# Attention and routed feed-forward layer: transposes in two steps, reciprocals spread by transfers, first scores in the projection stage

## The reference

```python
def xattn(Q, K, V):                       # Q = layernorm(x), K = V = context
    q = split_heads(Q @ Wq.T + bq); k = split_heads(K @ Wk.T + bk); v = split_heads(V @ Wv.T + bv)
    scores = einsum('bhqd,bhkd->bhqk', q, k) / sqrt(8)
    return merge(softmax(scores) @ v) @ Wo.T + bo
def ffn(xf):
    expert_idx = argmax(xf @ Wr.T + br)
    h = relu(einsum('td,efd->etf', xf, W1) + b1)
    y = einsum('etf,edf->etd', h, W2) + b2
    return y[expert_idx, arange(tokens)]
x = x + xattn(layernorm(x), ctx, ctx)
x = x + ffn(layernorm(x))
```

## Time and profile before

| | us |
|---|---|
| median of 3 runs | 499.29 (499.02 to 500.56) |
| the profiled execution, its own time | 501.58 |
| its span, first to last instruction | 499.8 |
| busy: PE, DVE, ACT, POOL | 461.1, 408.2, 313.0, 240.6 |

### The profile page before, as it was taken

How to read it: one execution, slowest core, us unless ns; L and a number is a source line. 1 busy time by engine, 2 the same in 40 slices (tenths; PEclk the granted TensorE clock), 3 DMA queues, 4 the chain that set the end, 5 groups by cost and what they waited for, 6 DMA issues and landing times. The chain is left out here.

```text
span 499.8 us, 18728 instructions
## 1 busy us (share of the span) xinstructions
PE 461.1 (92%) x6467; PEld 347.9 (70%) x6467; DVE 408.2 (82%) x1061; ACT 313.0 (63%) x589; POOL 240.6 (48%) x390
## 2 busy tenths in 40 slices
PE   3999978899999999999999999988789999999990
PEld 1666634456666666666666666668779999999990
DVE  4999864677899899998999999958878887887870
ACT  1677764666666666666666665665557777777760
POOL 1548620222232464555645645554767645455551
PEclk9999995999999999999999999999999999999996
DMA  8356300011000111111111115722223332222100
GB/s 281 108 148 177 90 11 12 14 22 20 18 17 18 33 41 30 38 38 36 35 34 33 39 41 201 264 71 76 77 66 103 101 87 66 72 61 74 39 32 0
DMA packets 32752, 33.98 MB, mean 68 GB/s; under 512 B 6675, under 2 KB 26006, under 8 KB 32416
## 3 DMA queue, kind: packets, MB, share of 16 engines
q1 hardware_dynamic: 27840, 24.10, 18.7%
q0 software_dynamic: 4832, 8.80, 5.3%
HBM read 19.14 MB, written 9.99 MB: 58 GB/s over the span
## 5 line engine op out<-in xcount | busy, mean ns | idle before, releaser
L451 POOL TENSOR_TENSOR VP<-BIG,C 128x128 f32<-128x128 f32 x128 | 56.1, 458 | 136.5 <-PE PS L1003 132.7
L918 PEld LDWEIGHTS PS<-C,SB 128*128 128x128 f32 x512 | 54.6, 142 | 68.2 <-ACT SB L546 32.5
L698 DVE TENSOR_REDUCE MX<-PS 128x16 f32<-128x1024 f32 x64 | 78.3, 1223 | 29.1 <-PE PS L877 27.7
L473 POOL DMA_INDIRECT out<-SB,BIG x71 | 70.1, 987 | 52.6 <-DVE SB L849 44.7
L918 PE MATMUL PS<-C,SB 128*128 128x128 f32 x512 | 85.1, 290 | 7.5 <-ACT PT L529 7.2
L546 ACT ACTIVATE SB<-SB 128x1024 f32<-128x1024 f32 x64 | 67.7, 1057 | 23.7 <-DVE SB L706 22.0
L706 DVE TENSOR_TENSOR SB<-PS,MX 128x1024 f32<-128x1024 f32 x64 | 77.4, 1210 | 1.7
L1024 PE MATMUL PS<-BIG,KM 128*128 128x128 f32 x568 | 76.8, 277 | 0.3 <-issue 0.2
L1037 PE MATMUL PS<-KM,SB 128*128 x568 | 75.8, 277 | 0.6 <-ACT SB L563 0.6
L466 POOL DMA_INDIRECT rows<-X,DESTI x64 | 64.2, 1003 | 19.6 <-issue 14.1
L877 PE MATMUL PS<-KM,BIG 64*64 64x512 f32 x512 | 71.2, 629 | 0.8 <-ACT BIG L517 0.8
(11 more groups left out here) (122 smaller groups left out, 699.0 us busy)
## 6 DMA issues: line engine op xcount, KB each, us to landing
BIG<-rows SPq DMA_DIRECT2D x71, 66.0 KB, 1.9
X<-in_x SPq DMA_DIRECT2D x16, 256.0 KB, 3.3
PT<-in_ctxT SPq DMA_DIRECT2D x16, 256.0 KB, 3.0
KM<-BIG SPq DMA_DIRECT2D x240, 16.0 KB
BIG<-in_we SPq DMA_DIRECT2D x1, 2576.0 KB, 11.5
KM<-in_w SPq DMA_DIRECT2D x1, 2048.0 KB, 15.9
out<-SB,BIG POOLq DMA_INDIRECT x71, 2.3
rows<-X,DESTI POOLq DMA_INDIRECT x64, 2.4
```

The costliest lines, as they stand in the source:

```text
L451: last = nc.gpsimd.tensor_tensor(dst, v, own, ALU.mult)
L473: nc.gpsimd.indirect_dma_start(out=out, out_offset=bass.IndirectOffsetOnAxis(ap=RT[:, s.r, ID:ID + 1].bitcast(i32), axis=0), in_=YO[:, s.r ...
L698: nc.vector.tensor_reduce(MX[:, n % 2, :], sc, axis=AX.X, op=ALU.max).then_inc(mx_done, 1)
L918: last = nc.tensor.transpose(bank(4)[:, i * P:(i + 1) * P], SB[:, n % 3, hp * P:(hp + 1) * P], ident)
```

## The change

Four things change.

- **Transposes in two steps.** The first half of a tile's transposes stays in PE's step n; the second half (and ACT's copy of it) moves to the head of step n + 1, ahead of the scores. The buffers of SB are turned by one so that the first tiles fit beside stage 1.
- **Reciprocals.** The selection matrix and its product go. SP writes the reciprocals of a group to a DRAM tensor `ratio` and reads them back with a broadcast into RDX; GpSimd multiplies them with NUM, and DVE no longer does. L_MUL and L_X1 grow to 9 and 10, and the routing steps move with them (SOON falls to 1).
- **First scores.** `scores(0)` moves from the last to the last but one group of stage 1 and `scores(1)` comes into the last group; Q and the transposes of the last group use other banks. The weights of Q and K have their columns turned (two ACT copies at the start), so that a head's rows lie at a stride and a group of KM takes 8 transfers of 16 rows.
- **Weight loads.** The loads of WE and W2 are issued by ACT, after its steps 58 and 61, instead of by SP. X1T has two slots instead of four.

```diff
-L_MUL = 8
-L_X1 = 9
+L_MUL = 9
+L_X1 = 10
-SOON = 2
+SOON = 1
...
+            def ratios(g):
+                sp.wait_ge(rd_done, g + 1)
+                need(sp, rdx_in[g % 2], 16 * (g // 2))
+                sp.dma_start(ratio[g % 2], RD[:, g % 2, :]).then_inc(rd_out[g % 2], 16)
+                need(sp, ot_ready, GT * (g - 1))
+                sp.wait_ge(rd_out[g % 2], 16 * (g // 2 + 1))
+                of = ratio[g % 2].rearrange("(h a) q -> h a q", a=DK)[:, 0:GT, :].rearrange("h t q -> h (t q)")
+                sp.dma_start(RDX[:, g % 2].rearrange("p t q -> p (t q)"), of.unsqueeze(1).to_broadcast([H, DK, GT * P])).then_inc(rdx_in[g % 2], 16)
+            for s in range(1, NG):
...
+                for j in range(HP):
+                    sp.dma_start(KM[j:P:HP, s % 2, j, :], KT[j:P:HP, s * GW:(s + 1) * GW]).then_inc(km_in[s % 2], 16)
+                if s >= 2:
+                    ratios(s - 2)
...
-            sp.dma_start(WE[:], we).then_inc(we_in, 16)
-            sp.wait_ge(s_done, NT - GT)
-            sp.dma_start(W2, w2).then_inc(w2_in, 16)
+            ratios(NG - 2)
...
             def masks(s):
+                m = s.n - L_MUL
+                if 0 <= m < NT:
+                    g, t = divmod(m, GT)
+                    pool.wait_ge(rdx_in[g % 2], 16 * (g // 2 + 1))
+                    pool.wait_ge(num_kept, m + 1)
+                    need(pool, wo_done, m - 1)
+                    nc.gpsimd.tensor_tensor(OT[:, m % 2, :], RDX[:, g % 2, t, :], NUM[:, m % 8, :], ALU.mult).then_inc(ot_ready, 1)
...
             def softmax(s):
                 n = s.n
+                if 3 <= n < NT + 3:
+                    act.wait_ge(pt_done, 2 * (n - 3) + 2)
+                    nc.scalar.copy(PT[:, (n - 3) % 2, 4:8, :].rearrange("p a b -> p (a b)"), bank(4)).then_inc(pt_ready, 1)
...
-                if 2 <= n < NT + 2:
-                    act.wait_ge(pt_done, 2 * (n - 2) + 2)
-                    nc.scalar.copy(PT[:, n % 2, 4:8, :].rearrange("p a b -> p (a b)"), bank(4)).then_inc(pt_ready, 1)
...
+                if n == NT - 6:
+                    for r in range(2):
+                        act.wait_ge(km_in[r], 16 * HP * (NG // 2 - 1 + r))
+                    act.dma_start(WE[:].rearrange("p e f -> p (e f)"), we.rearrange("p e f -> p (e f)"), max_dma_last_dim=2048).then_inc(we_in, 16)
...
-                m = n - L_MUL
-                if 0 <= m < NT:
-                    dve.wait_ge(num_kept, m + 1)
-                    nc.vector.tensor_tensor(OT[:, m % 2, :], bank(7)[:, 0:P], NUM[:, m % 8, :], ALU.mult).then_inc(ot_ready, 1)
...
+                if final:
+                    pe.wait_ge(q_kept, NG - 1)
+                    scores(1)
...
             def stage2(s):
                 n = s.n
-                if 1 <= n < NT:
+                m = n - 3
+                if 0 <= m < NT:
+                    pe.wait_ge(pt_ready, 2 * m + 1)
+                    transposes(m, 1)
+                if 2 <= n < NT:
...
-                    nc.tensor.matmul(bank(7)[:, 0:P], C[:, C_SEL + P * t:C_SEL + P * (t + 1)], RD[:, g % 2, :],
-                                     start=True, stop=True).then_inc(rdx_done, 1)
...
-                m = n - 2
-                if 0 <= m < NT:
-                    pe.wait_ge(pt_ready, 2 * m + 1)
-                    transposes(m, 1)
```

116 lines of the change are left out of this document (67 added, 49 removed).

## The result

The changed kernel takes **531.5 us** (median of 4 runs, 529.8 to 532.6) against 499.15 us of the kernel before (4 runs, 498.0 to 500.6): ratio 1.063, 95% interval 1.059 to 1.067. The forecast was 515.8 with a range to 527: slower was right, the size was half of what came. (Executions of one kernel differ by the clock that TensorE was granted: three of the four stand at a mean of 0.984 to 0.986 and took 531.4 to 532.6, the fourth at 0.992 and took 529.8.)

The account below looks back on a forecast made before the run. The prediction took bank 4, passed between PE and ACT, to set the step of stage 2. Terms +21.8, -1.1, -5.9 and +1.7 gave +16.5 on a 499.8 us span, 516.3, hence 515.8 us; range 509 to 522, wider 500 to 527.

Parts of the forecast that it names:

- Part 1: Stage 2 loop: moving second transposes to the next step closes a loop over three engines, 4.46 us a step, +21.8 us.
- S + 3.67 and S + 4.36: Stage 2: exponential starts 3.67 us after the start S of its scores, 4.36 where a reciprocal stands between maximum and subtraction.
- +21.8: Scores of tile 5 to the last: 7 steps at 3.96 and 51 at 4.46, 255.0 us against 233.2.
- The fourth change of the array's shape: PE's step in stage 2: four shape changes for three, the added one costing 0.20 us, held in the turn.
- Part 2: Reciprocals by transfer, product on GpSimd: worth 0 in stage 2, transfers of 6 to 7 us hidden; -1.1 us beside stage 3.
- -1.1: Steps 67 to 71, beside stage 3: the PE product that goes saves five times 0.22 us.
- Part 3: First scores: scores of tile 5 at 82.6 instead of 88.53, -5.9 us, with the clock holding in the fill.
- Part 4: Weight loads on ACT: the issue stands between exponential 58 and the copy the loop waits for, +1.7 us (0 to 4).
- (a): Rival: the loop does not bind, PE's own work decides near 3.75 us a step; 477 us, chance 0.11.
- (b): Rival: only the exponential's place counts in the loop, the X1T wait is hidden; 501 us, chance 0.09.
- (c): Rival: the clock falls in the fill all the same, +3.5 us; 519 us, chance 0.12.
- (d): Rival: reciprocal transfers late, GpSimd holds masks back and PE stands, two groups at 4 us; 524 us, chance 0.08.

Follow-up runs that it names:

- e16: Changed kernel with exponential a step later, sums before product with V, reciprocal a step earlier, batch work spread, last reciprocals issued earlier, weight loads on SP: 495.5 us, ratio 0.992.
- the mended order: Changed kernel with exponential later, sums first, reciprocal a step earlier, batch work spread, last reciprocals earlier: 496.5 us with weight loads on ACT, 495.5 on SP.
- five single edits: Changed kernel with exponential later, sums first, reciprocal before maximum, seed later or last reciprocals earlier, each alone: 525.6, 524.0, 535.5, 529.8, 529.9 us; all five: 499.1.
- e4: Changed kernel with VectorE's reciprocal moved ahead of the maximum: 535.5 us, ratio 1.071.
- e12: Changed kernel with exponential later, sums before product with V, reciprocal at the end of the step before, last reciprocals behind the second row load: 498.6 us, ratio 0.998.
- e8: Changed kernel with the seed of the inverse root one step later, GpSimd's roots in the step behind it: 529.8 us, ratio 1.058.

## Why the prediction was right or wrong, point by point

- **What bounds the loop** (Part 1): right. TensorE waits for the exponential and the copy behind it, the product with V for X1T, as forecast; three of four turns are within 0.13 us.
- **The step that failed in the loop** is "what runs beside this and is not late today: scores to exponential": the times S + 3.67 and S + 4.36 were carried over from before as if VectorE reached every maximum in time. They hold in three turns (in the turn above the exponential is 3.68 behind the scores of tile 42, 247.53 to 251.21) and not in the batch's: 252.37 to 257.42, 5.05. The sum's term for the loop was +21.8 and measured +28.7; 0.81 in the batch's turn, six times, is 5 of the missing 7, and some 0.1 in each other turn the rest. The diff showed the cause (L_X1 one up, M_SEED not). The term holds nothing for VectorE's batch work.
- **The fourth change of the array's shape**: the turn measured 3.30 against 3.23, with 0.20 and 0.17 idle ended by issue at the second transposes and at the scores. By the rule of the Trainium skill (TensorEngine Tiling (Array Packing), Key Properties) that switching the mode drains TensorE, these gaps belong to the turn, and the trace agrees: with a change of shape the first load starts 0.07 us before the modelled end of the matmuls ahead (251.79 against 251.86), without one 0.27 before (249.46 against 249.73). Without the added change the turn would have been 3.1.
- **Part 2**: "hidden" held in the loop, where GpSimd waited for the transfer once, 0.6 us. It held for the time at the end too, although GpSimd waited 5.65 us there: the product with WO started 10.5 us after the reciprocal (361.80 to 372.29) where 11.5 stood, and transfers and GpSimd's product took 7.5 of them. **The step that failed in the tail** is the term "-1.1" for "steps 67 to 71": it prices the product that goes and puts the step that comes at nothing. The tail measured +6.5, a miss of 7.6 us and larger than the loop's 6.9. In place of -1.1 the traces show the last tile's product with WO 6.2 us later at the full clock, 2.95 of it the added step, and about 2 us of lower clock; how the rest divides stays open. The round trip itself was sized right: 363.62 to 368.8 is 5.2 us where 6 to 7 stood. The Trainium skill (DMA: Bandwidth & Descriptors, Anatomy of one DMA — SWDGE (gpsimd) path) puts most of the some 2 us of fixed cost of a transfer that GpSimd issues into waiting for the write's receipt. Here SP issues, and 1.9 us lie between the issue of the 64 KB write and that of the read that waits for it, 365.52 - 363.62: the length is alike, how it divides the trace does not show.
- **Part 3**: right, -5.6 against -5.9; scores of tile 5 at 82.97 against 82.6, no slice at half clock. In all versions of the changed kernel they came at 81.3 to 84.4.
- **Part 4**: +1.7 was wrong, it measured 0.1 at most: the issue (0.44 and 0.39 us) lies beside the exponential that ACT is working on. The 1.57 of the earlier trace rows was no price of the load either: in e16 SP issues it, written as in before, in 0.42 us.
- **Rivals.** (a) does not apply to this order, but its mechanism, TensorE's own work at 3.75 a step, is what the mended order reached in its odd steps (3.78; 3.93 on average). (b) fell: X1T was waited for 28 times. (c) fell. (d) came true in one group, the last, as a wait of GpSimd's; with the clock held it cost nothing that the tails show (182.6 with it, 182.5 without).
- **What would show it**: scores came 4.59 us apart on average (tiles 12 to 63), where 4.4 to 4.5 stood. "GpSimd should never be waited for by PE" was broken, and "if PE waits for OT" came true: twice, 1.3 us, at the last two tiles.
- **Luck**: the price of 1.7 for the weight loads was an error that brought the sum nearer; without it the forecast would have been 514.1.

## What to carry to other kernels

A loop over several engines is as slow as its slowest closed path, and when several paths are nearly equal, mending one gives a part of its price or less than nothing: here five single edits gave 13 us in sum and all together 32. Test a suspected wait by leaving its edit out of the version where all are mended. And when a change shifts a step counter, list what else is counted from it and what is not: two blocks of small operations that used to stand in different steps can meet in front of the one operation that the loop needs. A step of latency added to a pipeline is hidden in its steady state and stands in its drain: count the steps from the last input to the last output, and give them a term of the sum.

## What the runs showed of the hardware

- The granted clock falls in the middle of a busy stage: in e4 2.59 us without weight loads were followed by loads at 1.5 to 2 times their duration (0.87 for 0.49, 0.76 for 0.38 or 0.43, 0.71 for 0.42, then 0.31 for 0.21 at 261.74); the granted clock is 0.50 from 259 to 261, the lower of the two levels, 1.2 GHz. So a late maximum cost more than its lateness: this step and the one ahead of it took 11.4 us (4.02 and 7.41) where after's two steps there take 10.0 (5.15 and 4.85).
- A small VectorE operation can last as long as a GpSimd instruction that runs beside it. The seed's operation on 128x8 integers (L782) takes 0.17 us in the first batch of after and in all six of e12, where no GpSimd instruction runs beside it. It takes 0.68 in the other five batches of after, where GpSimd issues a row transfer, and 0.31 in five of e16's (L777), where GpSimd makes its product; each time it ends with GpSimd's instruction, within 0.05 us:

```profile
252.99 1.01 POOL L486 DMA_INDIRECT rows<-X,DESTI  x1 [0.15 <-issue]
```
```profile
170.59 0.47 POOL L457 TENSOR_TENSOR OT<-RDX,NUM 128x128 f32<-128x128 f32 x1
170.79 0.31 DVE L777 TENSOR_SCALAR Y<-YY 128x8 int32<-128x8 int32 x1
```

  In e8, where the row transfer starts only 0.12 us ahead of the operation instead of 0.31, it takes 0.17. The Trainium skill (GPSIMD Engine Reference, Specifications) says that GpSimd shares its SBUF interfaces with VectorE, with contention where VectorE uses a mode of two ports or has two SBUF inputs; the durations agree with contention, but the trace does not name the mode, and no run took GpSimd's work alone away.
- An ACT instruction and a DMA issue from ACT's queue overlap fully (0.44 us at 324.93 and 0.39 us at 339.72, each beside a 1.06 us exponential). The issue of one load varies more than the queue explains: WE took 1.57 us on SP in before, 0.42 on SP in e16 and 0.44 on ACT in after.
